# The image stage of a fused vision-text block: the written orders of five engines are made anew, and small steps of VectorE change their operands or their engine

## The reference, cut to what matters

```python
h = tok(x)                                   # patches 768 -> 192, layernorm folded in, + pos
h = concatenate([h, txt], axis=1)            # 324 rows an image
# attention's place is taken by a state-space scan, 16 states a channel:
delta = softplus(xn @ W_1.T @ W_d.T + b_d)   # xn = layernorm(h)
state = exp(delta * A) * state + delta * B * xn      # along the 324 rows
h = h + sum_over_16_states(C * state)
# mixture of experts, on x2 = layernorm(h):
sig = sigmoid(x2 @ Wg.T); top 6 of 128 by sig + e_bias; weights sig / sum * 2.5
h = h + routed(x2) + silu(x2 @ Wsg) * (x2 @ Wsu) @ Wsd
```

## Time and profile before

| | |
|---|---|
| runs | 4209.94, 4213.53, 4214.15 us; median 4213.53 |
| the profiled execution | 4215.05 us, its span 4213.1 us, mean TensorE clock 0.967 |
| busy over the span | PE 90%, DVE 78%, POOL 72%, ACT 63% |
| image stage | to about 3180 us; bodies with all pieces from 282 to 2938 us |

### The profile page before, as it was taken

How to read it: one execution, slowest core, us unless ns; L and a number is a source line. 1 busy time by engine, 2 the same in 40 slices (tenths; PEclk the granted TensorE clock), 3 DMA queues, 4 the chain that set the end, 5 groups by cost and what they waited for, 6 DMA issues and landing times. The chain is left out here.

```text
span 4213.1 us, 74856 instructions
## 1 busy us (share of the span) xinstructions
PE 3809.9 (90%) x22114; PEld 2893.5 (69%) x22114; DVE 3271.8 (78%) x5523; ACT 2639.2 (63%) x4838; POOL 3019.3 (72%) x1609
## 2 busy tenths in 40 slices
PE   3469999999999999999999999998887999999998
PEld 2346666766666666666666666666556999999997
DVE  1788888888888888888888888888614777777774
ACT  1468888778888777888878788877641222222222
POOL 0887888887888888788788788888503666666665
PEclk8669999999999999999999999999998999999999
DMA  3333333333333333333333332332106888888886
GB/s 84 89 82 85 84 92 97 82 94 99 85 85 90 92 92 88 94 85 91 97 80 94 92 93 79 93 83 77 48 13 155 209 208 208 207 209 208 208 208 140
DMA packets 245582, 473.55 MB, mean 112 GB/s; under 512 B 41693, under 2 KB 164129, under 8 KB 245269
## 3 DMA queue, kind: packets, MB, share of 16 engines
q1 hardware_dynamic: 205840, 429.90, 38.0%
q0 software_dynamic: 36864, 37.98, 5.9%
q10 hardware_dynamic: 2564, 1.82, 0.2%
HBM read 404.99 MB, written 64.56 MB: 111 GB/s over the span
## 5 line engine op out<-in xcount | busy, mean ns | idle before, releaser
L508 POOL TENSOR_TENSOR y<-y,state 128x972 f32<-128x972 f32 x448 | 1015.0, 2266 | 340.2 <-DVE state L669 331.0
L487 POOL TENSOR_TENSOR state<-du,b_rows 128x972 f32<-128x972 f32 x512 | 1189.1, 2336 | 3.0
L663 DVE TENSOR_TENSOR_SCAN ps<-ps,state 128x972 f32<-128x972 f32 x512 | 1113.6, 2181 | 61.6 <-ACT ps L531 48.1
L531 ACT ACTIVATE ps<-delta,a_neg 128x324 f32<-128x324 f32 x1536 | 727.2, 521 | 320.2 <-DVE state L669 259.7
L669 DVE TENSOR_TENSOR state<-ps,c_rows 128x972 f32<-128x972 f32 x512 | 597.9, 1168 | 35.2 <-DVE ps L663 0.5
L1043 POOL DMA_INDIRECT out_rows<-yo,scatter_idx x256 | 369.5, 1443 | 298.0 <-DVE scatter_idx L1126 239.6
L783 PE MATMUL ps<-ws_d,inter 116*98 116x192 f32 (+1 forms) x3072 | 536.2, 328 | 17.7 <-issue 13.4
L783 PEld LDWEIGHTS ps<-ws_d,inter 116*98 116x98 f32 (+1 forms) x3072 | 498.4, 174 | 25.7 <-issue 18.8
L755 DVE TENSOR_TENSOR inter<-ag,ps 116x648 f32<-116x648 f32 x256 | 211.5, 826 | 314.2 <-PE ps L768 314.1
L765 PE MATMUL ps<-x2f,ws_u 128*116 128x324 f32 x1024 | 341.2, 456 | 51.3 <-ACT ag L639 49.3
L765 PE MATMUL ps<-x2f,ws_g 128*116 128x324 f32 x1024 | 335.8, 451 | 28.0 <-DVE inter L755 22.4
(11 more groups left out here) (174 smaller groups left out, 7339.0 us busy)
## 6 DMA issues: line engine op xcount, KB each, us to landing
b_rows<-bc_rows SPq DMA_DIRECT2D x256, 324.0 KB, 5.0
c_rows<-bc_rows SPq DMA_DIRECT2D x256, 324.0 KB, 5.6
w_lo<-in_we_up SPq DMA_DIRECT2D x128, 348.0 KB
w_down<-in_we_down SPq DMA_DIRECT2D x128, 336.0 KB
x_in<-in_x SPq DMA_DIRECT2D x32, 1176.0 KB, 7.9
w_hi<-in_we_up SPq DMA_DIRECT2D x256, 116.0 KB
image_cnt<-running_counts SPq DMA_DIRECT2D x256, 81.0 KB
w_lo<-in_we_up SPq DMA_DIRECT2D x128, 116.0 KB
```

The source lines that it names most:

```text
L487: nc.gpsimd.tensor_tensor(b.state[n % 4][:], b.du[t.p][:], row, ALU.mult).then_inc(input_ready, 1)
L508: nc.gpsimd.tensor_tensor(y, y, b.state[n % 4][:], ALU.add).then_inc(y_added, 1)
L531: ins = nc.scalar.activation(to[:, c * L:c * L + L], b.delta[t.p][:, c, :], ACT.Exp, scale=b.a_neg[:, c, k:k + 1])
L663: nc.vector.tensor_tensor_scan(s, s, b.state[k % 4][:].rearrange("p a t -> p (a t)"), 0.0, ALU.mult, ALU.add).then_inc(scan_done, 1)
```

## The change

It does four things. (1) All five lists of `ORDER` are new. Scans 12 to 15 of a pair, their fill_c and up_u (3,5) to (3,7) now open DVE's next body, ahead of choose; on PE up_u (3,7) opens the body, on ACT silu (3,7), then softplus of the pair whose scans begin; POOL's fills from fill_b 10 and fill_c 8 on move to its next body too. find and find_a move behind. SP loads the second quarter of C for the next pair at the end of its body and the first quarter of B at its beginning. (2) eps is added to the variance of both layernorms by ACT (Identity with a bias), and so is the guard of the six weights' sum, with the factor 1 / 2.5 in it; DVE takes one reciprocal of that (piece factor). The three DVE additions and products at L706, L739 and L741 go. (3) The Newton steps keep their intermediate values in PSUM, in 52 columns beside the area of a scan that is still open (`held`); the step has three multiplications and one last instruction, and for the layernorms that last one is done twice, into SBUF and into PSUM. (4) emb_stats keeps its intermediates there too.

The lists of PE, ACT and DVE after the change, and the edits outside the lists:

```diff
     "pe": (
-        ("down_a", 3, 0), ("down", 3, 0), ("resid", 1, 0), ("down_a", 3, 1), ("down", 3, 1), ("resid", 1, 1), ("down_a", 3, 2), ("down", 3, 2),
...
-        ("up_u", 2, 5), ("step", -1, 1), ("up_g", 2, 6), ("warm", 2, 5), ("step", -1, 2), ("up_u", 2, 6), ("warm", 2, 6), ("up_g", 2, 7), ("warm", 2, 7),
-        ("up_u", 2, 7), ("warm", 1, 0)
+        ("up_u", 3, 7), ("warm", 3, 5), ("down_a", 3, 0), ("down", 3, 0), ("warm", 3, 7), ("down_a", 3, 1), ("down", 3, 1), ("resid", 1, 0),
+        ("up_g", 2, 0), ("resid", 1, 1), ("down_a", 3, 2), ("count", 2, 0), ("down", 3, 2), ("up_u", 2, 0), ("resid", 1, 2), ("emb_a", -2, 0),
+        ("count", 2, 1), ("up_g", 2, 1), ("warm", 2, 3), ("emb", -2, 0), ("up_u", 2, 1), ("warm", 2, 1), ("warm", 2, 2), ("x2_turn", 1, 0),
+        ("up_g", 2, 2), ("warm", 3, 4), ("x2_turn", 1, 1), ("emb_a", -2, 1), ("up_u", 2, 2), ("emb", -2, 1), ("up_g", 2, 3), ("x2_turn", 1, 2),
+        ("up_u", 2, 3), ("x1_turn", -1, 0), ("up_g", 2, 4), ("x1_turn", -1, 1), ("x1_turn", -1, 2), ("up_u", 2, 4), ("bc_values", -1, 0),
+        ("up_g", 2, 5), ("gate", 1, 0), ("step", -1, 0), ("up_u", 2, 5), ("find", 2, 0), ("gate", 1, 1), ("up_g", 2, 6), ("step", -1, 1),
+        ("up_u", 2, 6), ("step", -1, 2), ("up_g", 2, 7), ("warm", 1, 0), ("warm", 2, 6)
     "act": (
-        ("decay", 0, 0), ("decay", 0, 1), ("down", 3, 0), ("decay", 0, 2), ("emb_a", -2, 0), ("resid", 1, 0), ("down", 3, 1), ("decay", 0, 3),
...
-        ("decay", 0, 15), ("step", -1, 1), ("up_g", 2, 6), ("to_exp", 2, 6), ("step", -1, 2), ("softplus", -1, 0), ("up_g", 2, 7), ("to_exp", 2, 7)
+        ("up_g", 3, 7), ("to_exp", 2, 0), ("softplus", 0, 0), ("down", 3, 0), ("emb_a", -2, 0), ("decay", 0, 0), ("emb_stats", -1, 0),
+        ("decay", 0, 1), ("to_exp", 2, 1), ("to_exp", 3, 7), ("resid", 1, 0), ("down", 3, 1), ("decay", 0, 2), ("decay", 0, 3), ("den", 2, 0),
+        ("resid", 1, 1), ("up_g", 2, 0), ("decay", 0, 4), ("down", 3, 2), ("count", 2, 0), ("decay", 0, 5), ("to_exp", 2, 3), ("resid", 1, 2),
+        ("decay", 0, 6), ("count", 2, 1), ("ln2_stats", 1, 0), ("up_g", 2, 1), ("ln2_apply", 1, 0), ("to_exp", 2, 2), ("emb_a", -2, 1),
+        ("decay", 0, 7), ("x2_turn", 1, 0), ("emb", -2, 0), ("up_g", 2, 2), ("ln1_stats", -1, 0), ("decay", 0, 8), ("x2_turn", 1, 1),
+        ("ln1_apply", -1, 0), ("decay", 0, 9), ("up_g", 2, 3), ("emb", -2, 1), ("x2_turn", 1, 2), ("decay", 0, 10), ("x1_turn", -1, 0),
+        ("up_g", 2, 4), ("x1_turn", -1, 1), ("to_exp", 2, 4), ("x1_turn", -1, 2), ("decay", 0, 11), ("decay", 0, 12), ("bc_values", -1, 0),
+        ("up_g", 2, 5), ("gate", 1, 0), ("to_exp", 2, 5), ("step", -1, 0), ("decay", 0, 13), ("decay", 0, 14), ("gate", 1, 1), ("up_g", 2, 6),
+        ("step", -1, 1), ("to_exp", 2, 6), ("decay", 0, 15), ("step", -1, 2)
     "dve": (
-        ("choose", 2, 0), ("choose", 2, 1), ("choose", 2, 2), ("scan", 0, 0), ("fill_c", 0, 0), ("scan", 0, 1), ("fill_c", 0, 1), ("scan", 0, 2),
...
-        ("fill_c", 0, 14), ("up_u", 2, 6), ("emb_stats", -2, 0), ("scan", 0, 15), ("fill_c", 0, 15), ("up_u", 2, 7)
+        ("scan", 1, 12), ("fill_c", 1, 12), ("up_u", 3, 5), ("scan", 1, 13), ("scan", 1, 14), ("fill_c", 1, 13), ("up_u", 3, 6), ("fill_c", 1, 14),
+        ("scan", 1, 15), ("fill_c", 1, 15), ("up_u", 3, 7), ("choose", 2, 0), ("choose", 2, 1), ("choose", 2, 2), ("weigh", 2, 0), ("scan", 0, 0),
+        ("scan", 0, 1), ("fill_c", 0, 0), ("fill_c", 0, 1), ("weigh", 2, 1), ("scan", 0, 2), ("factor", 2, 0), ("fill_c", 0, 2), ("scan", 0, 3),
+        ("fill_c", 0, 3), ("scan", 0, 4), ("up_u", 2, 0), ("fill_c", 0, 4), ("ln2_stats", 1, 0), ("scan", 0, 5), ("ln2_apply", 1, 0),
+        ("emb_scale", -1, 0), ("fill_c", 0, 5), ("up_u", 2, 1), ("scan", 0, 6), ("ln1_stats", -1, 0), ("fill_c", 0, 6), ("scan", 0, 7),
+        ("ln1_apply", -1, 0), ("fill_c", 0, 7), ("up_u", 2, 2), ("scan", 0, 8), ("fill_c", 0, 8), ("scan", 0, 9), ("emb_stats", -2, 0),
+        ("up_u", 2, 3), ("fill_c", 0, 9), ("scan", 0, 10), ("fill_c", 0, 10), ("up_u", 2, 4), ("scan", 0, 11), ("fill_c", 0, 11), ("find_a", 2, 0),
+        ("find", 2, 0)
...
+def held(piece):
+    before = [(kind, k) for kind, _, k in ORDER["dve"]]
+    before = before[:before.index(piece)]
+    open_scans = [k for kind, k in before if kind == "scan" and ("fill_c", k) not in before]
+    return open_scans[-1] % 2
...
+                    elif kind == "den":
+                        act.wait_ge(den_summed, t.v + 1)
+                        nc.scalar.activation(b.top8[:, :, 1], b.top8[:, :, 0], ACT.Identity, bias=b.small[:, 1:2], scale=1.0 / SCALE).then_inc(den_scaled, 1)
                     elif kind in ("ln1_stats", "ln2_stats"):
                         m = int(kind[2]) - 1
+                        act.wait_ge(ln_mean[m], t.v + 1)
+                        nc.scalar.activation(stat[:, m + 1, 4, :], b.mean_var[m][:, :, 1], ACT.Identity, bias=b.small[:, 0:1]).then_inc(ln_var[m], 1)
                         rsqrt_guess(m + 1, 128, 6, ln_var[m], ln_log[m], ln_r0[m], t)
...
-            def newton(m, rows, cols, link):
+            def newton(m, rows, cols, piece, link, to):
                 s = stat[0:rows, m, :, 0:cols]
-                link(nc.vector.tensor_tensor(s[:, 0, :], s[:, 5, :], s[:, 5, :], ALU.mult))
-                link(nc.vector.scalar_tensor_tensor(s[:, 1, :], s[:, 0, :], -0.5, s[:, 4, :], ALU.mult, ALU.mult))
-                link(nc.vector.scalar_tensor_tensor(s[:, 3, :], s[:, 1, :], 1.5, s[:, 5, :], ALU.add, ALU.mult))
-                return s[:, 3, :]
+                p = [spare[held(piece)][0:rows, 8 * q:8 * q + cols] for q in range(4)]
+                link(nc.vector.tensor_scalar(p[0], s[:, 5, :], -0.5, None, ALU.mult))
+                link(nc.vector.tensor_tensor(p[1], p[0], s[:, 5, :], ALU.mult))
+                link(nc.vector.tensor_tensor(p[2], p[1], s[:, 4, :], ALU.mult))
+                if to is None:
+                    nc.vector.scalar_tensor_tensor(s[:, 3, :], p[2], 1.5, s[:, 5, :], ALU.add, ALU.mult)
+                    to = p[3]
+                link(nc.vector.scalar_tensor_tensor(to, p[2], 1.5, s[:, 5, :], ALU.add, ALU.mult))
+                return to
...
-                        link(ins)
-                        nc.vector.tensor_scalar(stat[:, m + 1, 4, :], b.mean_var[m][:, :, 1], EPS, None, ALU.add).then_inc(ln_var[m], 1)
+                        ins.then_inc(ln_mean[m], 1)
...
-                        link = Chain(dve, "weigh", t, (0, 1)[k])
                         den = b.top8[:, :, 0]
                         if k == 0:
                             dve.wait_ge(mask_ready, t.v + 1)
-                            link(nc.vector.scalar_tensor_tensor(b.ch[:], b.gt[:], 1.0, b.mask[:], ALU.add, ALU.mult))
+                            Chain(dve, "weigh", t)(nc.vector.scalar_tensor_tensor(b.ch[:], b.gt[:], 1.0, b.mask[:], ALU.add, ALU.mult))
                         else:
-                            link(nc.vector.tensor_reduce(den, b.ch[:], AX.X, ALU.add))
-                            link(nc.vector.tensor_scalar(den, den, 2e-20, None, ALU.add))
-                            link(nc.vector.reciprocal(b.top8[:, :, 1], den))
-                            nc.vector.tensor_scalar(b.x2[:, :, :, D], b.top8[:, :, 1].rearrange("p (b k) -> p b k", b=2), SCALE, None, ALU.mult).then_inc(factor_ready, 1)
+                            nc.vector.tensor_reduce(den, b.ch[:], AX.X, ALU.add).then_inc(den_summed, 1)
+                    elif kind == "factor":
+                        dve.wait_ge(den_scaled, t.v + 1)
+                        nc.vector.reciprocal(b.x2[:, :, :, D], b.top8[:, :, 1].rearrange("p (b k) -> p b k", b=2)).then_inc(factor_ready, 1)
```

More of the change, by code:

```diff
@@ L76 @@
[L76 to L79, removed]
@@ L85 @@
-        ("ln2_stats", 1, 0), ("scan", 0, 5), ("find_a", 2, 0), ("ln2_apply", 1, 0), ("emb_scale", -1, 0), ("fill_c", 0, 5), ("up_u", 2, 1),
-        ("ln1_stats", -1, 0), ("find", 2, 0), ("scan", 0, 6), ("ln1_apply", -1, 0), ("fill_c", 0, 6), ("scan", 0, 7), ("fill_c", 0, 7), ("up_u", 2, 2),
-        ("scan", 0, 8), ("fill_c", 0, 8), ("scan", 0, 9), ("up_u", 2, 3), ("fill_c", 0, 9), ("scan", 0, 10), ("fill_c", 0, 10), ("up_u", 2, 4),
-        ("scan", 0, 11), ("fill_c", 0, 11), ("scan", 0, 12), ("fill_c", 0, 12), ("scan", 0, 13), ("fill_c", 0, 13), ("up_u", 2, 5), ("scan", 0, 14),
@@ L97 @@
+        ("fill_b", 0, 4), ("fill_b", 0, 5), ("fill_c", 0, 2), ("fill_b", 0, 6), ("fill_c", 0, 3), ("fill_c", 0, 4), ("fill_c", 0, 5),
+        ("fill_b", 0, 7), ("fill_b", 0, 8), ("fill_c", 0, 6), ("fill_b", 0, 9), ("fill_c", 0, 7)
     ),
     "sp": (
-        ("load_b", 0, 1), ("load_x", -2, 0), ("store_out", 3, 0), ("store_out", 3, 1), ("load_c", 0, 1), ("load_b", 0, 2), ("store_out", 3, 2),
-        ("load_txt", -1, 0), ("store_mid", 2, 0), ("load_b", 0, 3), ("load_c", 0, 2), ("load_c", 0, 3), ("bc_values", -1, 0), ("load_b", -1, 0),
@@ L101 @@
-        ("load_c", -1, 0)
```

(9 more changed lines are left out.)

38 lines of the change are left out of this document (16 added, 22 removed).

## The result

The kernel after the change takes 4278.9 us (median; 4270.3 to 4282.1), the one before 4212.5 beside it. The ratio is 1.0155, 95% interval 1.0137 to 1.0173: 66 us slower, where 43 less were predicted, and outside the range. The profiled execution took 4278.3 us, its span is 4276.3.

The account below looks back on a forecast made before the run. A cycle of PE's part, then ACT's, bounds the kernel: 33.9 + 0.2 + 55.0 = 89.1 us, 90.1 on average with the branch; 1.4 saved in 31 bodies, 43 us off 4213.1, gives 4170 us, 8-in-10 range 4110 to 4235.

Parts of the forecast that it names:

- the new order's handshakes cost another microsecond: Rival "nothing happens": waits for ACT's evictions and a silu leave bodies at 91.2 to 91.6, 4205 to 4222 us; chance 0.14.
- the wait at up_u (2,6): On PE, within the no-change rival (0.14): up_u (2,6) waits for a silu behind gate 1's extra table load.
- the sum's own assumption that TensorE waits for nothing behind count: From count (2,1) to silu (3,7) only ACT's part, 55.0 us, was summed, with no TensorE wait added.
- PE's 1.2 and ACT's stop lie before up_u (3,7), at the same place of the cycle, so the larger counts: At the loop branch: PE's stop 1.2 us, ACT's between 1.2 and 2.3, up to 3.1; 2.0 taken.
- The two parts: Body cut at count (2,1): PE from up_u (3,7), 33.9 us, then ACT to silu (3,7), 55.0 us.
- 20 loads a body: Sign on ACT: 20 table loads in each body, 15 of them from count on.
- the third rival's chain: Rival "slower": softplus over 3.1 us late delays decays, resid 1, silu (2,0), up_u (2,0); about 4260 us, chance 0.20.
- The small steps: DVE loses four tensor_scalars that stop for POOL: about 5 us a body off the cycle, worth nothing at once.
- the surcharge of 65 ns: DVE instructions with PSUM operands, by the Trainium skill: some 18 at 65 ns, 1.2 us a body.
- No wait for the silu at up_u (2,0): Sign on PE: a wait for the silu at up_u (2,0) would show the prediction wrong; cover there 3.1 us.
- Alternation: Sign: bodies with and without a branch become 91 and 89 us; still 4 us apart would show the prediction wrong.
- the first rival: Rival "more is saved": bodies of 87.4 us, 126 us less, some 4088, half giving 4140; chance 0.20 for below 4145.

Follow-up runs that it names:

- all of it: Changed kernel with one warm moved, table loads cut, SyncE's loads away from the branch, and TensorE's and ScalarE's branches moved: 0.9810 of the kernel before, 4133.6 us.

## Why the prediction was wrong

**The step that failed** is "the new order's handshakes cost another microsecond", the price of the wait at up_u (2,6), together with the sum's own assumption that TensorE waits for nothing behind count. The wait was seen, with its right cause, and put among the rivals with chance 0.14. It is 1.22 us long and costs 67 us over the kernel, 4.7 for two steady bodies (188.0 to 183.3). The moved warm shows it (-67 us with every load in place), and the single load behind which the silu stood, taken out with every warm in its place, shows it again (-77). Its price is what follows: half clock over three pieces, 3.25, and a TensorE that comes late to the branch.

**The branch.** "PE's 1.2 and ACT's stop lie before up_u (3,7), at the same place of the cycle, so the larger counts" failed in two ways. TensorE's stop is 3.99 and not 1.2, since the trace of before showed it under conditions that the change took away: a piece issued ahead, and no loads. And the larger does not count but the later: where the clock had fallen TensorE entered its stop 3.25 us late, and on average the stop ended 3.2 us behind the silu. With TensorE on time ScalarE's stop counts, as said, at 2.9 instead of 2.0.

**The two parts were right.** 33.9 for TensorE's: 34.1 where the clock is full (all of it, with branch). 55.0 for ScalarE's: 54.8, and 20 loads a body. Softplus behind silu (3,7) did not come too late: all of TensorE's waits for silus at up_u come to 40.5 us in 28 bodies, 1.4 each, which up_u (2,6) with 1.22 nearly uses up; the third rival's chain was not what made it slower:

```profile
L793 PE MATMUL ps<-x2f,ws_u 128*116 128x324 f32 x900 | 317.1, 478 | 90.9 <-ACT ag L662 40.5 <-issue 39.9 <-PE ps L813 7.4
```

**The small steps** were priced at nothing. In the old lists they bring 39 us, and in the new ones the kernel's ratio is 1.0819 without them and 1.0155 with them. VectorE's waits for TensorE, 201 us in 29 bodies, say that VectorE is early there; they do not say that it is early everywhere, for scans feed ScalarE's decay, which also stands in the cycle. The price of a PSUM operand was taken rightly at 0.17; the surcharge of 65 ns that the prediction set beside it does not show (0.16 to 0.17 with PSUM operands, 0.16 to 0.17 on SBUF ones that nothing stopped).

**Signs named.** 20 loads: yes. VectorE's small instructions below 0.3: means of 0.14 to 0.17, yes. No wait for the silu at up_u (2,0): yes. The guards on ScalarE: 0.30 each and not 0.2. Alternation: "still 4 us" was to show the prediction wrong, and it is 4.8. Softplus ends 94.1 apart and not 90.1; bodies of 89 and 91: no.

**Slips in the working.** Half of the 126 us of the first rival would give 4150, not 4140, and the multiply's row has 826 ns, not 829. Neither changes the forecast.

**What stays open.** Even with the warm moved the change stands at 0.9996, 4211 us, 41 above the predicted 4170, 3.1 for two bodies. 0.8 of it is in ScalarE's part with the branch, 2.2 in TensorE's parts: behind a branch that is 35.7 in bodies where the clock falls at the stop and 34.2 where it doesn't, and in the other body 35.1, which I did not take apart. Why the clock falls behind the wait of 1.22 in 12 of 13 bodies with a branch and in 4 of 13 without stays open. That queue q8 carries the instructions that TensorE waits for at a stop is read from the packet's time and its kind; no run changed the fetch alone, and what makes the packet start early or late, other than the loads and what stands ahead of the branch, is not shown.

## What to carry to other kernels

Ask of each wait of TensorE not how long it is but how thin the work around it is: one microsecond of waiting at the end of a stretch of short pieces can cost the clock for the pieces behind it, and a dummy matmul moved into the wait can be worth more than any cut of work. Take the price of a stop at a loop's branch only together with what stands ahead of it and what transfers are under way, and expect it to change when these do. Where two engines stop at the same place, work out which one ends last, and with what delay it gets there.
